# Edge network of a two-layer graph kernel: four buffers, whole-block vector work, a three-level node search for six columns at once, nodes as 128 by 98

## The reference, cut to what matters

```python
h = relu(layernorm(x))
# layer 0: gated MLP on the edge features, summed per destination
m = silu(silu(edge_attr @ W1 + b1) @ W2 + b2) * sigmoid(silu(edge_attr @ G1 + g1) @ G2 + g2)
x = x + h + segment_sum(m, dst, 12500)
# layer 1: attention over the incoming edges
h = relu(layernorm(x))
s, r = h @ Ws + bs, h @ Wr + br            # 4 heads of 16
logits = einsum('ehd,d->eh', mish(s[src] + r[dst]), aw) + ab
alpha = softmax of logits over the edges with one dst
x = x + segment_sum(alpha * s[src], dst, 12500)
```

## Time and profile before

| | us |
|---|---|
| median of 3 runs | 6303.33 (6302.56 to 6303.81) |
| the profiled execution | 6302.94 |
| its span, first to last instruction | 6301.1 |
| busy: VectorE, POOL, ACT, TensorE | 4619.8, 3544.2, 2838.6, 1251.4 |
| edge_mlp, from the start to the last copy of rows | 0 to 1690.6 |
| update_nodes, first gather to last scatter | 1719.7 to 2032 |
| attention | 2037 to 6124 |
| finish | 6129 to 6301 |

### The profile page before, as it was taken

The page is one execution under the profiler, slowest core; times in us unless marked ns, Lnnn a source line. Parts: engine busy times, 40 slices in busy tenths (PEclk is TensorE's granted clock), DMA queues, the critical chain, the costliest instruction groups (busy, mean ns, idle before and its releaser), DMA issues. The chain is left out here.

```text
span 6301.1 us, 45975 instructions
## 1 busy us (share of the span) xinstructions
PE 1251.4 (20%) x8389; PEld 527.7 (8%) x8389; DVE 4619.8 (73%) x4935; ACT 2838.6 (45%) x3154; POOL 3544.2 (56%) x3660
## 2 busy tenths in 40 slices
PE   5666677777521000000000000000000000000000
PEld 2222222322221000000000000000000000000000
DVE  6777776666653687778778877887778777878771
ACT  4555555666400444444444444444444444444430
POOL 1111110000087777777777777777777777777757
PEclk8889888888855555555555555555555555555555
DMA  5556555555422223322332232223322332232211
GB/s 170 185 182 186 181 184 173 169 167 172 145 53 57 68 79 83 86 79 79 87 82 79 79 90 80 79 79 83 86 79 79 88 82 79 79 90 79 79 56 44
DMA packets 317016, 655.20 MB, mean 104 GB/s; under 512 B 114338, under 2 KB 114340, under 8 KB 316747
## 3 DMA queue, kind: packets, MB, share of 16 engines
q1 hardware_dynamic: 188153, 508.07, 25.2%
q0 software_dynamic: 126720, 146.75, 11.1%
q10 hardware_dynamic: 2128, 0.23, 0.0%
HBM read 415.07 MB, written 239.34 MB: 104 GB/s over the span
## 5 line engine op out<-in xcount | busy, mean ns | idle before, releaser
L873 POOL DMA_INDIRECT se<-s_proj,idx x3168 | 2992.5, 945 | 965.4 <-issue 959.6
L891 ACT ACTIVATE held_ps<-r_keep 128x1536 f32 (+1 forms) x135 | 196.3, 1454 | 1463.3 <-DVE z L974 1423.7
L1112 PE MATMUL a_ps<-r_ident,r_state 128*4 128x128 f32 x1 | 0.4, 375 | 4125.9 <-DVE drop L1141 4125.9
L974 DVE TENSOR_TENSOR z<-se,held_ps 128x1536 f32<-128x1536 f32 x135 | 369.9, 2740 | 454.6 <-DMA se<-s_proj,idx 417.5
L308 ACT ACTIVATE hidden<-h_ps,r_b1g 128x1024 f32<-128x1024 f32 x404 | 450.3, 1115 | 468.9 <-PE h_ps L258 468.0
L258 PE MATMUL h_ps<-edges,r_w1g 64*64 64x512 f32 x3232 | 540.7, 737 | 417.3 <-DMA edges<-in_edge_attr 401.4
L362 DVE SCALAR_TENSOR_TENSOR msg<-gate,value 128x512 f32<-128x512 f32 x404 | 277.0, 686 | 450.0 <-ACT gate L317 436.8
L489 POOL DMA_INDIRECT block_of<-in_dst,block_id x106 | 105.7, 997 | 844.8 <-DVE block_id L396 844.8
L938 ACT ACTIVATE arows<-work_ps 128x1632 f32<-128x1632 f32 x135 | 206.8, 1532 | 740.8 <-DVEq L1010 740.8
L999 DVE TENSOR_TENSOR wse<-se,ex_ps 128x1536 f32<-128x1536 f32 x135 | 373.6, 2767 | 201.3 <-ACT ex_ps L929 201.3
L378 DVE TENSOR_TENSOR_SCAN sums<-keepb,sums,msg 128x512 f32<-128x512 bf16 x403 | 515.7, 1280 | 7.1
(11 more groups left out here) (180 smaller groups left out, 4313.0 us busy)
## 6 DMA issues: line engine op xcount, KB each, us to landing
states<-arows SPq DMA_DIRECT2D x135, 864.0 KB, 6.9
rs<-sums SPq DMA_DIRECT2D x135, 768.0 KB, 5.2
edges<-in_edge_attr SPq DMA_DIRECT2D x202, 512.0 KB, 4.3
sums<-rows SPq DMA_DIRECT2D x402, 256.0 KB, 2.6
keepb<-keep SPq DMA_DIRECT2D x404, 128.0 KB, 2.9
se<-s_proj,idx POOLq DMA_INDIRECT x3168
x_tile<-in_x SPq DMA_DIRECT2D x10, 312.5 KB
s_proj<-sr SPq DMA_DIRECT2D x10, 312.5 KB
```

The lines of the kernel that those rows point to most:

```text
L873: pool.indirect_dma_start(out=se[b][:, k, :], out_offset=None, in_=D["s_proj"], in_offset=bass.IndirectOffsetOnAxis(ap=node[:, k:k + 1], a ...
L974: nc.vector.tensor_tensor(z[b][:, :, :], se[b][:, :, :].rearrange("p k f -> p f k"), rneg, ALU.subtract).then_inc(z_ready, 1)
```

## The change

It touches the edge block, the shape of the nodes and nothing in attention but what follows from that shape.

- Edges, flags and sums get four buffers (block c in buffer c mod 4). SP's order per block becomes: load edges of c + 4, store the rows of c - 2, load the flags of c + 3.
- Product, scan and copy to rows work on whole blocks of 1024 columns. `value`, `gate` and `msg` are 1024 wide, still two of each. TensorE and ACT still work in halves. The transposes of block c - 2 come after layer 1 of block c + 1.
- The search has three levels (75 samples, then 55, then 100 entries) and does six columns in one instruction. The compare and the sum are two instructions now, written to `below` in between. An iteration is four blocks; it has the third level of group i - 2 after its first block, the second level of group i - 1 after its second, the first level of group i after its third. 17 groups of six make 102 columns.
- POOL fetches six times per level (rows of 55 and of 100 entries). In its loop it waits for the first level of group q, issues six fetches for it, then waits for the second level of group q - 1 and issues six.
- The sample gather is 75 by 55 elements; a second table `firsts` has one in 55 of them. SP does both after the flags.
- The 23 small operations (25 now) stand before the last four blocks.
- Nodes are 128 by 98: update_nodes and finish have 14 steps of JB = 7 columns. The host pads x to 12544 rows and cuts the output.

```diff
-NP, NJ = 125, 100
-JB = 10
+NP, NJ = P, 98
+NN = NP * NJ
+JB = 7
+JQ = (4, 3)
-SB, SL, SP_ = 750, 550, 125
-NC = CH - 2
+S1, S2, S3 = 75, 55, 100
+Q = 6
+NC = 102
...
-        edges = [sb(f"edges{b}", [P, BLK]) for b in range(2)]
+        edges = [sb(f"edges{m}", [P, BLK]) for m in range(4)]
...
-        NI = NBLK // 2
-        QI = NC // 2
+        NI = (NBLK - 2) // 4
+        NQ = NC // Q
...
+            def step(c, m, first=False, last=False):
+                if not last:
+                    sp.wait_ge(h_ready, (c + 1) * 2)
+                    load(c + 4, m)
+                if not first:
+                    store(c - 2, m % 2)
+                if not last or c + 3 < NBLK:
+                    wait(sp, scanned, c)
+                    sp.sem_inc(sp_turn, 1)
+                    load_keep(c + 3, (m + 3) % 4)
             load(0, 0)
-            sp.dma_start(sample[:, :], dst.rearrange("(p a k) -> p a k", p=SP_, k=SL)[:, :, 0], **one).then_inc(sample_in, 16)
+            load(1, 1)
+            sp.dma_start(sample[:, :], dst.rearrange("(p a k) -> p a k", p=S1, k=S3)[:, :, 0], **one).then_inc(sample_in, 16)
...
+            def step(c, m, round, first=False, last=False):
+                for u in range(2):
+                    layer2(c, u)
+                    if not last:
+                        layer1(c + 1, (m + 1) % 4, u, round + (m + 1) // 4)
+                if not first:
+                    turn_rows(c - 2, (m + 2) % 4)
...
+            def count(rows, counts, q, size, n):
+                cols = bass.ds(q * Q, Q)
+                node = nid[:, cols].unsqueeze(2).to_broadcast([P, Q, size])
+                wait(dve, counted, n - 1)
+                nc.vector.tensor_tensor(below[:, :, 0:size], rows, node, ALU.is_le).then_inc(below_ready, 1)
+                dve.wait_ge(below_ready, n)
+                nc.vector.tensor_reduce(counts[:, cols], below[:, :, 0:size], AX, ALU.add).then_inc(counted, 1)
+                dve.wait_ge(counted, n)
...
+            def search(i, j, first, second, third, n):
+                if third and j == 0:
+                    find_third(i - 2, n + 1)
+                if second and j == 1:
+                    find_second(i - 1, n + third + 1)
+                if first and j == 2:
+                    find_first(i, n + third + second + 1)
+            def body(i, n, first=False, second=False, third=False):
+                early = isinstance(i, int) and i == 0
+                for j in range(4):
+                    step(i * 4 + (2 + j), (2 + j) % 4, i + j // 2, i * 2 + j // 2, second=early and j < 2)
+                    search(i, j, first, second, third, n)
+            def step(c, m, round, pair, first=False, second=False):
+                product(c, m % 2)
+                if not first:
+                    to_rows(c - 2, m % 2, pair, first=second)
+                scan(c, m, round, first=first and m == 0)
...
-            with pool.Fori(0, QI) as i:
-                for b in range(2):
-                    fetch_block(i * 2 + b, b)
+            blocks3 = A["dst"].rearrange("(a k) -> a k", k=S3)
+            fetch(0, nodes2, D["samples"], block1, block1_known, nodes2_in)
+            with pool.Fori(1, NQ) as q:
+                fetch(q, nodes2, D["samples"], block1, block1_known, nodes2_in)
+                fetch(q - 1, nodes3, blocks3, block2, block2_known, nodes3_in)
+            fetch(NQ - 1, nodes3, blocks3, block2, block2_known, nodes3_in)
```

More of the change, by code:

```diff
@@ L229, in _ @@
             sp.wait_ge(keep_out, 16)
-            load_keep(0, 0)
-            load_keep(1, 1)
+            for c in range(3):
+                load_keep(c, c)
+            sp.wait_ge(sample_in, 16)
+            sp.dma_start(D["samples"], sample[:, :]).then_inc(sample_out, 16)
+            sp.dma_start(D["firsts"].rearrange("(p a) -> p a", a=1), sample[:, 0:1], **one).then_inc(sample_out, 16)
+            sp.wait_ge(sample_out, 32)
+            sp.dma_start(samples[:, :], row(D["firsts"]).to_broadcast([P, S1])).then_inc(samples_in, 16)
@@ L232, in _ @@
             sp.wait_ge(zeros_ready, 1)
             sp.dma_start(D["sums"][E:P * RUN, :].rearrange("(p k) f -> p (k f)", p=PAD_P), zeros[0:PAD_P, 0:PAD]).then_inc(pads_out, 16)
-            body(0, first=True)
-            with sp.Fori(1, NI - 1) as i:
-                body(i)
-            body(NI - 1, last=True)
+            for c in range(2):
+                step(c, c, first=True)
+            with sp.Fori(0, NI - 1) as i:
+                for j in range(4):
+                    step(i * 4 + (2 + j), (2 + j) % 4)
@@ L252, in layer1 @@
                 wait(pe, hidden_ready, n - 1)
                 pe.sem_inc(pe_turn, 1)
-                for m in range(2):
-                    out, cols = slice(F * m, F * m + F), slice(F * m, F * m + F)
+                for k in range(2):
+                    units = slice(F * k, F * k + F)
                     for s in range(2):
                         feats = slice(F * s, F * s + F)
-                        last = nc.tensor.matmul(h_ps[u % 2][out, s, :], R["w1g1"][feats, cols], edges[b][feats, half], start=True, stop=True)
+                        last = nc.tensor.matmul(h_ps[u][units, s, :], R["w1g1"][feats, units], edges[m][feats, half], start=True, stop=True)
@@ L291, in _ @@
             pe.wait_ge(weights_in, 16 * WEIGHTS)
-            layer1(0, 0)
-            layer1(0, 1)
+            layer1(0, 0, 0, 0)
+            layer1(0, 0, 1, 0)
             pe.wait_ge(ident_steps, 2)
-            body(0, first=True)
-            with pe.Fori(1, NI - 1) as i:
-                body(i)
-            body(NI - 1, last=True)
-            turn_rows(NBLK - 1, (NBLK - 1) % 2)
+            for c in range(2):
+                step(c, c, 0, first=True)
+            with pe.Fori(0, NI - 1) as i:
+                for j in range(4):
+                    step(i * 4 + (2 + j), (2 + j) % 4, i + j // 2)
@@ L301, in _, with hid @@
+            for j in range(4):
+                step(NBLK - 4 + j, (2 + j) % 4, NI - 1 + j // 2, last=j == 3)
+            for c in range(NBLK - 2, NBLK):
+                turn_rows(c, c % 4)
         @block.scalar
         def _(act):
-            def hid(i, u):
-                i, u = i + u // 4, u % 4
-                n = i * 4 + u
+            def hid(c, u):
+                n = c * 2 + u
                 act.wait_ge(h_ready, n + 1)
                 wait(act, g_ready, n - 1)
-                nc.scalar.activation(hidden[u % 2][:, :, :], h_ps[u % 2][:, :, :], ACT.Silu, bias=R["b1g1"][:, :]).then_inc(hidden_ready, 1)
@@ L316, in outs, with step @@
                 act.wait_ge(g_ready, n + 1)
-                nc.scalar.activation(gate[u % 2][:, :], g_ps[:, :], ACT.Tanh, scale=0.5, bias=g2[:, :]).then_inc(gated, 1)
-            def body(i, last=False):
-                for u in range(4):
-                    if not (last and u + 1 >= 4):
-                        hid(i, u + 1)
-                    outs(i, u)
+                nc.scalar.activation(gate[b][:, half], g_ps[:, :], ACT.Tanh, scale=0.5, bias=g2[:, :]).then_inc(gated, 1)
+            def step(c, m, last=False):
+                hid(c, 1)
+                outs(c, m % 2, 0)
+                if not last:
+                    hid(c + 1, 0)
+                outs(c, m % 2, 1)
@@ L349, in _ @@
             hid(0, 0)
-            body(0)
-            with act.Fori(1, NI - 1) as i:
-                body(i)
-            body(NI - 1, last=True)
+            for c in range(2):
+                step(c, c)
+            with act.Fori(0, NI - 1) as i:
+                for j in range(4):
+                    step(i * 4 + (2 + j), (2 + j) % 4)
+            for j in range(4):
+                step(NBLK - 4 + j, (2 + j) % 4, last=j == 3)
             act.wait_ge(later_in, 16 * 9)
```

269 lines of the change are left out of this document (126 added, 143 removed).

## The result

The kernel after takes 5891.26 us (median of four runs, 5890.82 to 5892.57), the kernel before beside it 6302.94 (6296.54 to 6303.81). The ratio is 0.9349, with a 95% interval of 0.9333 to 0.9365. Forecast were 5925 us and a range of 5825 to 6040. The span went from 6301.1 to 5889.5, so 411.6 us are to be found in the stages.

What follows compares the result with a forecast made beforehand. Edge stage bound by one transfer in every other block, update and finish by POOL's issue. Edge stage -297, update -55, finish -27, attention zero: -379 on 6302.9 gives 5925 us, range 5825 to 6040.

Steps and rivals of the forecast that it cites:

- Block price: Edge stage outside the search: chain of ACT gate, layer 2, value, gate, plus transposes, costs 5.55 us a block.
- VectorE outside the search: Edge stage: product 1.23, rows 1.22, scan 2.33 us, less overlap 4.6 us a block, hidden behind 5.55.
- The third level waits for POOL: Search: nodes3 fetches queue behind nodes2's, so the third compare waits 12 to 14 us in 16 iterations.
- the wait of 23.1 us: Search: block known to twelfth fetch landed, with fetches locked by VectorE; gives a period of 37.2 us per four blocks.
- rival 1: Search: no lock of fetches by VectorE, wait 18.3 us, 77 us less, 5848 us; chance 0.12.
- start: Edge stage start: sample gather issue 5.6 us, keep loads delayed 3; first scan at 37 us, first(1) done at 80.
- Rest of the edge stage: After the last third-level wait: restart 5.3, 129 blocks 716, small operations 2.5, tail 8.5 us; stage ends at 1393.
- Update and finish: Gathers and scatters on 128 partitions, 196 and 98 of them: update 258 us (-55), finish 122.5 us (-27).
- rival 6: Attention: its gather interval grows; 0.117 us each eats all 379, +0.24 gives 6703 us; chance 0.03.
- Rival 3: Update and finish: the 1.2 us per fetch is not a matter of partitions; +72, 5997 us; chance 0.07.
- Rival 4: Edge stage: transfers stay the bound, later blocks keep 7.69 us; 276 us more, 6201 us; chance 0.06.
- Rival 2: Search: nothing waits for POOL, fetches land within two steps; 23.4 us per iteration, 5704 us; chance 0.04.

Runs made afterwards that it cites:

- the split: Against the kernel with POOL's rounds exchanged and small tables written earlier: four transposes after layer 1 of each half, rows copied before the product; 5666.39 us, ratio 0.8985.
- the exchanged rounds: Against the kernel after: POOL's loop issues the six fetches of nodes3(q-1) before the six of nodes2(q); 5722.08 us, ratio 0.9081.
- the node shape alone: Against the kernel before: only the nodes as 128 by 98, with 14 steps of 7 columns; 6207.19 us, ratio 0.9852.
- the widths: Against the kernel after: the finish's seven gathers per step on 128, 127, 126, 125, 120, 96 and 64 partitions; single run in the second batch, 6470.78 us.
- the second batch: Second of three batches of four runs, each on a different chip with its own run of the kernel before, here 6807.1 us.
- the unsplit one: Against the kernel after: POOL's rounds exchanged and samples and firsts written before the wait for flags; 5718.11 us in the third batch.

## Why the prediction was right, and where its sizes were off

The result lies in the range, 34 us below the forecast, and the forecast's own case came true. By its steps:

- **Block price**: 5.55 forecast, 5.53 measured over 119 blocks. That the gate chain with its transposes makes it is shown by the split: 5.08 with intervals of 2.54. With two buffers for edges it is 6.59.
- **VectorE outside the search**: product 1.222, rows 1.217, scan 2.342 us against 1.23, 1.22 and 2.33. It stays hidden, busy 551 of 660 us.
- **The third level waits for POOL**: 16 waits, as forecast, of 11.2 us instead of 12 to 14. That the queue order makes them, and not the fetches as such, is shown by the exchanged rounds.
- **Mis-sized: the wait of 23.1 us** in "I walk it through". It was 20.45, and the period 34.44 instead of 37.2 (607.25 less 90.7 in 15 periods): 15 x 2.76 + 2.8 = 44 us too much. Two things were off. The landing took 2.7 us (from the start of the last fetch, 348.94, to the compare, 351.64), where I took 3.7 of the earlier trace rows, from fetches of 550 entries a row, where these have 100. And the walk held every fetch that began in a scan to its end and then charged it in full, 0.94; it is charged 0.76, and one that begins 0.07 after the scan's start isn't held. So the twelfth fetch went out 17.75 after block known, not 19.4. This charge could be read before, and I misread it:

```profile
171.66 0.69 DVE L362 SCALAR_TENSOR_TENSOR msg<-gate,value 128x512 f32<-128x512 f32 x1 [0.33 <-issue]
...
172.14 1.03 POOL L489 DMA_INDIRECT block_of<-in_dst,block_id  x1 [9.91 <-DVE block_id L396]
```

  In the kernel before, 50 of the 106 fetches began 0.33 to 0.49 us into a product like this one and ended 0.82 us after it. I took the mean of 0.997 to show little, because the fetches mostly met no scan, and kept rival 1 at 0.12 for it; nearly half of them were held, only briefly. The lock itself is real: without it 18.3 less the landing's 1.0 would be 17.3, and 20.45 was measured.
- **Mis-sized: start**. The first scan came at 30.3 instead of 37: the sample gather took 1.10 us to issue, not 5.6, and the keep loads weren't held up by four edge loads. But first(1) ended at 90.7 instead of 80. What I had not seen is that SP waits there for the two small tables, with load(4) queued behind: 12.85 us of TensorE, and 19.5 us from the third scan to the fourth where I had one block. Those first three scans also took 8.7 us from first to third instead of 3.6. Net 10.7 us too little. I had asked what is queued behind a waiting instruction for POOL, but for SP's start only what the transfers themselves cost.
- **Rest of the edge stage**: 627.5, the last third, to 1360.9 is 733.4 us; 5.3 + 716 + 2.5 + 8.5 = 732.3 were forecast. Together -44 + 10.7 + 1.1 = -32, which is 1360.9 against 1393.
- **Update and finish**: 256.1 and 122.6 against 258 and 122.5; attention's gathers 0.945 unchanged, so rival 6 didn't come. Rival 3 (not a matter of partitions) is refuted by the node shape alone and by the widths.
- **Rival 1** (no lock, 5848) and the forecast (5925) lie on both sides of 5891, so the total could not part them; the rows of held fetches do. **Rival 4** (transfers stay the bound) is what the kernel would be nearer to with two buffers for edges: 6.59 us a block. **Rival 2** (nothing waits for POOL, 5704) is where the kernel is with the exchanged rounds: 5722. I had tied it to an interval of 0.4 us; a change of order reached it at an interval of 1.25.

The version with exchanged rounds, earlier tables, split transposes and rows first takes 5666.39 us: 0.8985 of the kernel before, where the kernel after has 0.9349.

## What to carry to other kernels

When an engine's queue serves two producers of a loop, order its requests as their results are needed, and count how many steps lie between each request and its use: here the later-needed six fetches stood first and cost 169 us. Choose the number of partitions of an indirect DMA by its divisors and pad (128 rather than 125, and not 127; 64, 96 and 120 were as cheap as 128). Where one chain of two engines sets the pace, spread side work (the transposes) evenly over its turns, and check that its own inputs are ready there.

## What the hardware showed that I had not expected

- An indirect DMA costs POOL 2.56 us on 127 partitions, 1.21 on 125, 0.99 on 126, and 0.92 to 0.97 on 128, 120, 96 and 64.
- A fetch is held by a VectorE instruction only if it begins more than about 0.1 us after that instruction (0.08 wasn't held, 0.13 was). It then ends 0.75 to 0.82 after it, less than its 0.94 in full. Beside dummy work that repeats every 1.25 us, as the fetches do, the two fall into step and the hold doesn't show after the first.
- In the second batch the kernel before took 6807 us instead of 6303, and the split kernel 6246 instead of 5666. Of the split kernel's 579 us, some 508 lie in attention (4555 us instead of 4047), 37 in the update and 22 in the edge stage. These are waits of the widths kernel, 2000 to 5000 us (total, times, longest). The kernel after has neither: ACT's held_ps waits for VectorE alone there.

```profile
ACT held_ps L936 <- issue: 550.9, 63, 11.4
...
DVE rnew L1006 <- issue: 147.5, 60, 4.6
```

  Instructions kept their lengths (the work_ps scan 3.57 us in both), but ACT and VectorE paused with nothing that the profile shows to release them, and POOL waited for VectorE. The edge stage of the widths kernel, whose code is that of the kernel after, ended at 1361.1 there, as on the other chip (1360.9). What the pauses are stays open; no run tells it. The stretched iterations of 25.2 us misled me, and so the split kernel was run again beside the unsplit one.
